# Cross attention: softmax sums by bf16 products of a split sum tile, taken four slots behind the pass

## Chip, cores, metric

One core of a Trainium2 chip. The metric is the device time of one execution in microseconds. The kernel computes a whole decoder of two layers; the change touches the cross attention of the second one.

## The reference, cut to what matters

The cross attention of layer 1 has 4 batch rows of 256 query tokens, 16 query heads in 4 groups of key and value heads, head size 128, and 1857 keys (the 256 tokens themselves and 1601 of context). Queries and keys are projected, normalised and rotated. Then, per head:

```python
scores = jnp.einsum('bhqd,bhkd->bhqk', q, k) * SCALE
p = softmax(scores)                       # over the 1857 keys
out = jnp.einsum('bhqk,bhkd->bhqd', p, v)
x = x + out.reshape(B, S, H * HD) @ Wo.T
```

The kernel divides by the softmax sum at the end: what a head adds to x is multiplied by one over the sum of its exponentials.

## The kernel before, in words

The stage "stream" (`cross_stream`, line 1705 on) makes 32 **passes** (4 batch rows x 4 key heads x 2 halves, each half 2 query heads x 256 queries = 512 columns). A pass has 15 **steps**, one per tile of 128 keys (the last has 65). All engines run the same hand-written list of **slots**, one step a slot; each kind of work for step s stands in slot s plus a fixed delay, and every engine works its list in order:

- slot s: TensorE (PE) makes the scores of step s, three bf16 products of 512 columns (L1950), into bank s % 2. ScalarE (ACT) copies them to SBUF (L2038), into one of 22 rooms. VectorE (DVE) takes the running maximum (L2217, L2214 for the first two tiles) from the bank, and that frees the bank: the score of step s + 2 waits for the maximum of step s.
- 15 to 17 slots behind a pass's first: the maximum is transposed (L1958), reduced (L2235) and spread over a bank (L1965).
- slot s + 18: DVE lowers step s by the maximum (L2203), ACT takes its exponential (L2044).
- slot s + 20: GpSimd (POOL) adds the exponentials of step s to `acc`, an fp32 tile of 128x512, two of them by turns (L2145, L2142); PE multiplies them with the values (fp32, L1975) into bank 2 or 3, the bank of the weighed values of this pass.
- slot 15h + 35 and 36 of pass h: ACT and DVE split the weighed values in two bf16 halves, `att` (L2086, L2271).
- slot 15h + 36: PE sums `acc` over its partitions (`sum_up`, L1983): four fp32 products with a column of ones, each 128 weights wide and one column long, into bank 6. The profile shows each as two records. DVE takes the reciprocal (L2277). The last pass has a form of its own (L1989).
- slots 15h + 40 and 41: PE multiplies `att` with the output weights (L2004), DVE adds to x with the reciprocals (L2288). Bank 6 is shared by the transposed maxima, turned queries and keys, sums and output products, each waiting until the one before it is taken.

Between these, every five slots a **unit** of the next key head's projections begins: products in slots 0 to 3 of the unit (L1893), ACT's squares (L2054) and copies of the values (L2070), DVE's rotations (L2262, L2263), POOL's sums and norms (L2152, L2158, L2163), and later the transposes (L1935), ACT's L2080 and DVE's L2267. The pattern of slots repeats every two passes, so even and odd passes see different neighbours.

Wo is loaded in the first four groups through `raw`, a tile of 128x1024 fp32: 4 loads of 512 KB on SP's queue (`out_weights`), each split by ACT (L2115) and in two parts by DVE (L2329). Context chunks (`ctx_chunk`) share the queue.

Of the kernel before, what the change touches and what calls it, by code (L numbers as in the profile page):

```python
# [8 lines left out]
ALU = mybir.AluOpType  # L9
# [1576 lines left out]
SUM_LATE = ATT_LATE + 1  # L1586
OUT_LATE = 2 * STEPS + 10

# [45 lines left out]
def cross_attention(nc, x, const, a, w, kept, first_row, experts):  # L1634

    with Stage(nc, "cross") as keep:
# [6 lines left out]
        less = sb("less", [P, P], BF16)  # L1643
        half = sb("half", [P, 4])
# [5 lines left out]
        with Stage(nc, "cross_w") as st:  # L1650
# [8 lines left out]
            with nc.Block() as block:  # L1659
                @block.gpsimd  # L1660
                def _(gp):
                    nc.gpsimd.memset(ones[:], 1.0)
                    nc.gpsimd.memset(less[:], -1.0)
                    nc.gpsimd.memset(half[:], -0.5)
                    nc.gpsimd.memset(eps[:], 1e-6)
# [35 lines left out]
        cross_stream(nc, x, const, a, w, experts, w_q, w_kv, w_o, k_gain, q_gain, freq, ones, less, half, eps, own_t, in_t, ctx_t,  # L1701
# [3 lines left out]
def cross_stream(nc, x, const, a, w, experts, w_q, w_kv, w_o, k_gain, q_gain, freq, ones, less, half, eps, own_t, in_t, ctx_t,  # L1705
                 where, where_f, angle, turns, sin, k_tab, q_tab, raw):

    with Stage(nc, "stream") as st:
# [17 lines left out]
        raw_o = raw[:].rearrange("p (h n) -> p h n", h=REP)  # L1726
# [120 lines left out]

        with nc.Block() as block:
            @block.sync
            def _(sp):  # L1850
                def out_weights(k):
                    if k >= 1:
                        sp.wait_ge(wo_lo, 2 * k)
                    sp.dma_start(raw_o, w["Wo"].rearrange("(k h p) n -> k p h n", p=P, h=REP)[k]).then_inc(wo_loaded, 16)
# [7 lines left out]
                for b in range(1, BATCH):  # L1862
# [20 lines left out]
            def _(pe):  # L1883
# [83 lines left out]
                def weigh(step):  # L1967
# [5 lines left out]
                    if t == 0 and h >= 2:  # L1973
                        pe.wait_ge(att_lo, h - 1)
                    nc.tensor.matmul(ps[:, 2 + n, :], v[0:r, g % 2, t, :], room(step)[0:r],  # L1975
                                     start=(t == 0), stop=(t == KT - 1)).then_inc(weighed, 1)

                def sum_up(h):
                    wait_bank6("sum", h)
                    if h < LAST:  # L1980
                        pe.wait_ge(acc_ready, after_first(STEPS * (h + 1) - 1))
                        for c in range(4):
                            last = nc.tensor.matmul(ps[:, 6, c:c + 1], acc[:, h % 2, c * P:(c + 1) * P], ones[:], start=True, stop=True)  # L1983
                    else:
                        pe.wait_ge(acc_ready, after_first(STEPS * h + REST - 1))
# [733 lines left out]
```

## Time and profile before

| | us |
|---|---|
| median of 3 runs | 1640.0 |
| lowest, highest | 1637.98, 1640.43 |
| profiled execution | 1639.1 |
| its span, first to last instruction | 1637.1 |

The stream runs from about 460 to 1556 us of the span. Times in the rows are microseconds from the span's start unless marked ns. PE is the matmuls, PEld the weight loads of the same engine, which can run beside earlier matmuls. In the timelines the first number is the start, the second the time until the end; consecutive matmuls overlap in their tails, so the distance between two starts is what a matmul costs the engine. A bracket at the end is idle time of the engine and what ended it.

### The profile page before, as it was taken

How to read it: one execution, taken by the hardware profiler on the slowest of the kernel's cores; microseconds unless marked ns; L12 is line 12 of the kernel's file. 1: busy time of each engine (PE TensorE's matmuls, PEld its weight loads, DVE VectorE, ACT ScalarE, POOL GpSimd, SP SyncE). 2: the span in 40 equal slices, each digit the busy share in tenths (PEclk: the TensorE clock that was granted, in tenths of full speed). 3: DMA queues.
4: the chain of work that ended last, by engine and by line, in shares of the span. 5: the costliest groups of instructions: out<-in, count | busy, mean ns of one | idle time of the engine just before them, and what ended most of it. 6: DMA issues, size and time to landing. Idle time of an engine off the chain costs nothing. (4 is left out here: it accounts for less than half of the span.)

```text
span 1637.1 us, 25648 instructions
## 1 busy us (share of the span) xinstructions
PE 1462.8 (89%) x8204; PEld 847.8 (52%) x8204; DVE 1305.8 (80%) x2612; ACT 1022.6 (62%) x2407; POOL 1133.5 (69%) x1034
## 2 busy tenths in 40 slices
PE   6598697758779999899999999989989999999988
PEld 5477465433444555455455555545545555554455
DVE  7876576878669888888978888888888888888865
ACT  3364464744366877677677767677666766767552
POOL 2364462112458889988878998878899888887742
PEclk9799798879899999999999999999999999999999
DMA  3000841020100001000000000000000000000020
GB/s 103 1 3 2 280 133 39 1 74 0 33 1 14 12 3 35 20 1 1 1 1 1 28 14 1 1 1 1 14 28 1 1 1 1 1 1 0 1 59 27
DMA packets 30974, 38.45 MB, mean 23 GB/s; under 512 B 4980, under 2 KB 26488, under 8 KB 30840
## 3 DMA queue, kind: packets, MB, share of 16 engines
q1 hardware_dynamic: 30840, 36.82, 7.0%
q8 instruction: 66, 1.08, 0.3%
q14 instruction: 68, 0.56, 0.1%
HBM read 35.76 MB, written 1.05 MB: 22 GB/s over the span
## 5 line engine op out<-in xcount | busy, mean ns | idle before, releaser
L2145 POOL TENSOR_TENSOR stream_acc<-stream_acc,stream_weights 128x512 f32<-128x512 f32 (+1 forms) x374 | 491.9, 1315 | 74.2 <-ACT stream_weights L2044 52.3
L1975 PE MATMUL stream_banks<-stream_weights,stream_v 128*128 128x512 f32 (+1 forms) x876 | 450.0, 598 | 0.0
L2038 ACT COPY stream_weights<-stream_banks 128x512 f32<-128x512 f32 (+1 forms) x438 | 255.8, 584 | 226.7 <-PE stream_banks L1950 216.8
L2217 DVE TENSOR_TENSOR stream_most<-stream_most,stream_banks 128x512 bf16<-128x512 bf16 (+1 forms) x416 | 284.7, 684 | 138.4 <-ACT stream_weights L2038 124.0
L2044 ACT ACTIVATE stream_weights<-stream_weights 128x512 f32<-128x512 f32 (+1 forms) x438 | 278.0, 635 | 66.6 <-DVE stream_weights L2203 62.8
L2203 DVE TENSOR_TENSOR stream_weights<-stream_weights,stream_banks 128x512 f32<-128x512 f32 (+1 forms) x438 | 296.8, 680 | 1.9 <-PE stream_banks L1965 0.6
L1950 PE MATMUL stream_banks<-stream_q_t_hi,stream_k_t_hi 128*128 128x512 bf16 (+1 forms) x480 | 183.1, 381 | 15.4 <-DVE stream_most L2217 13.9
L2152 POOL TENSOR_TENSOR stream_by_cos<-stream_by_cos,stream_by_sin 128x256 f32<-128x256 f32 x192 | 135.8, 728 | 79.0 <-DVE stream_by_sin L2263 79.0
L1950 PE MATMUL stream_banks<-stream_q_t_hi,stream_k_t_lo 128*128 128x512 bf16 (+1 forms) x480 | 182.8, 381 | 0.0
L1950 PE MATMUL stream_banks<-stream_q_t_lo,stream_k_t_hi 128*128 128x512 bf16 (+1 forms) x480 | 182.8, 381 | 0.0
L1975 PEld LDWEIGHTS stream_banks<-stream_weights,stream_v 128*128 128x128 f32 (+1 forms) x876 | 145.2, 191 | 29.8 <-issue 4.3
L1950 PEld LDWEIGHTS stream_banks<-stream_q_t_lo,stream_k_t_hi 128*128 128x128 bf16 (+1 forms) x480 | 47.5, 99 | 138.8 <-issue 135.0
L1950 PEld LDWEIGHTS stream_banks<-stream_q_t_hi,stream_k_t_hi 128*128 128x128 bf16 (+1 forms) x480 | 47.2, 98 | 138.2 <-issue 102.5
L2163 POOL TENSOR_TENSOR stream_normed<-stream_by_cos,row_ctx_t 128x512 f32<-128x512 f32 x96 | 100.1, 1043 | 8.4 <-PE stream_banks L1935 1.1
L2054 ACT ACTIVATE stream_squares<-stream_banks 128x128 bf16<-128x128 f32 x368 | 96.7, 276 | 8.2 <-PE stream_banks L1893 8.0
L2158 POOL TENSOR_TENSOR row_ctx_t<-row_ctx_t,cross_half 128x4 f32<-128x4 f32 x96 | 100.4, 1046 | 0.0
L1893 PE MATMUL stream_banks<-early_w_kv_hi,row_in_t_hi 128*128 128x256 bf16 x416 | 79.5, 273 | 5.1 <-DVE stream_by_sin L2263 5.1
L1893 PE MATMUL stream_banks<-early_w_kv_lo,row_in_t_hi 128*128 128x256 bf16 x416 | 79.5, 273 | 0.0
L1893 PE MATMUL stream_banks<-early_w_kv_hi,row_in_t_lo 128*128 128x256 bf16 x416 | 79.4, 273 | 0.0
L2054 ACT ACTIVATION_READ_ACCUMULATOR stream_squares<-stream_banks 128x1 f32 x368 | 76.9, 209 | 0.0
L1950 PEld LDWEIGHTS stream_banks<-stream_q_t_hi,stream_k_t_lo 128*128 128x128 bf16 (+1 forms) x480 | 47.4, 99 | 56.8 <-issue 0.8
L1893 PEld LDWEIGHTS stream_banks<-early_w_kv_hi,row_in_t_hi 128*128 128x128 bf16 x416 | 40.2, 98 | 52.5 <-DVE stream_by_sin L2263 7.1
(443 smaller groups left out, 3097.6 us busy)
## 6 DMA issues: line engine op xcount, KB each, us to landing
memory_raw_t<-in_ctx_t SPq DMA_DIRECT2D x4, 1601.0 KB, 8.9
memory_raw<-in_ctx SPq DMA_DIRECT2D x4, 1536.0 KB
row_ctx_t<-in_ctx_t SPq DMA_DIRECT2D x6, 512.0 KB, 3.6
early_raw<-in_L_xattn_Wq SPq DMA_DIRECT2D x4, 512.0 KB, 3.8
early_raw<-in_L_xattn_Wo SPq DMA_DIRECT2D x4, 512.0 KB, 3.9
row_ctx_t<-in_ctx_t SPq DMA_DIRECT2D x1, 1601.0 KB, 6.9
moe_raw_up<-in_L_ffn_wi SPq DMA_DIRECT2D x6, 256.0 KB, 4.9
model_x<-in_x SPq DMA_DIRECT2D x1, 1024.0 KB, 5.6
```

The costliest lines, as they stand in the source:

```text
L1893: last = nc.tensor.matmul(out, rows, moving(two, c), start=(n == 0), stop=(n == 3 * DC - 1))
L1950: last = nc.tensor.matmul(ps[0:r, step % 2, :], k_t[one][:, t * P:t * P + r], q_t[two][:, g % 2, PAIR * n:PAIR * (n + 1), :], start=(one = ...
L1975: nc.tensor.matmul(ps[:, 2 + n, :], v[0:r, g % 2, t, :], room(step)[0:r], start=(t == 0), stop=(t == KT - 1)).then_inc(weighed, 1)
L2038: nc.scalar.copy(room(step)[0:r], ps[0:r, step % 2, :]).then_inc(copied, 1)
L2044: nc.scalar.activation(room(step)[0:r], room(step)[0:r], ACT.Exp, scale=SCALE).then_inc(p_ready, 1)
L2054: last = nc.scalar.activation(squares[:, h, :], heads[:, h - some.start, :], ACT.Square, accum_out=ss[:, u % 2, h:h + 1])
L2145: nc.gpsimd.tensor_tensor(acc[0:r, h % 2, :], acc[0:r, h % 2, :], room(step)[0:r], ALU.add).then_inc(acc_ready, 1)
L2152: last = nc.gpsimd.tensor_tensor(by_cos[:, u % 2, 0:n, to], by_cos[:, u % 2, 0:n, to], by_sin[:, u % 2, 0:n, of], ALU.add)
L2158: nc.gpsimd.tensor_tensor(rms[:, u % 2, 0:n], var[:, u % 2, 0:n], half[:, 0:n], ALU.pow).then_inc(rms_ready, 1)
L2163: nc.gpsimd.tensor_tensor(normed[:, 0:n], by_cos[:, u % 2, 0:n], bcast(rms[:, u % 2, 0:n], 2, HD), ALU.mult).then_inc(normed_ready, 1)
L2203: nc.vector.tensor_tensor(room(step)[0:r], room(step)[0:r], ps[0:r, 7, :], ALU.add).then_inc(lowered, 1)
L2217: nc.vector.tensor_tensor(most[0:r], most[0:r], ps[0:r, step % 2, :], ALU.max).then_inc(maxed, 1)
```

## The change

The sum of a pass h < 31 is now made from two bf16 halves of `acc`. In slot 15h + 38 ACT copies `acc` to a bf16 tile and DVE subtracts it from `acc` into a second one, the rounding rest. In slot 15h + 39 PE makes eight bf16 products with a bf16 column of ones, two per 128 queries, accumulated, into the bank of the weighed values of the pass (2 or 3), which `att` has freed by then. The reciprocal moves to the same slot, and the next pass but one waits for it before it weighs into that bank. Bank 6 no longer holds sums, but for the last pass's. The two halves lie in the second half of `raw`, so that Wo now comes in 8 loads of 256 KB through the first half, and its splits and their slots move (ACT at slots 8 and 17 of a group, DVE at 12 and 22). ACT's `split_high` stands right behind its exponential of the slot, DVE's `split_low` right behind its running maximum.

```diff
+SPLIT_LATE = SUM_LATE + 2
+def sums_in(slot):
+    return [h for h in pass_at(slot, SPLIT_LATE + 1) if h < PASSES - 1] + [h for h in pass_at(slot, SUM_LATE) if h == PASSES - 1]
+def splits_in(slot):
+    found = [("sum", h) for h in pass_at(slot, SPLIT_LATE) if h < PASSES - 1]
+    return found
...
-        raw_o = raw[:].rearrange("p (h n) -> p h n", h=REP)
+        raw_o = raw[:, 0:512].rearrange("p (h n) -> p h n", h=2)
+        halves = [raw[:, 512 + 256 * i:768 + 256 * i].bitcast(BF16) for i in range(2)]
...
-                                ("sum", pass_at(s, SUM_LATE)), ("out", outs_in(s))):
+                                ("sum", sums_in(s)), ("out", outs_in(s))):
                 for item in items:
-                    if kind == "out" and item[0] == PASSES - 1:
+                    if kind == "out" and item[0] == PASSES - 1 or kind == "sum" and item < PASSES - 1:
                         continue
...
                 def out_weights(k):
                     if k >= 1:
-                        sp.wait_ge(wo_lo, 2 * k)
-                    sp.dma_start(raw_o, w["Wo"].rearrange("(k h p) n -> k p h n", p=P, h=REP)[k]).then_inc(wo_loaded, 16)
+                        sp.wait_ge(wo_lo, k)
+                    sp.dma_start(raw_o, w["Wo"].rearrange("(k h p) n -> k p h n", p=P, h=2)[k]).then_inc(wo_loaded, 16)
...
                     if b == 1:
-                        out_weights(1)
-                        out_weights(2)
+                        for k in range(1, 6):
+                            out_weights(k)
                     ctx_chunk(b, 2)
                     if b == 1:
-                        out_weights(3)
+                        out_weights(6)
                     ctx_chunk(b, 3)
+                    if b == 1:
+                        out_weights(7)
...
                     if t == 0 and h >= 2:
                         pe.wait_ge(att_lo, h - 1)
+                        pe.wait_ge(inv_ready, h - 1)
...
                 def sum_up(h):
-                    wait_bank6("sum", h)
                     if h < LAST:
-                        pe.wait_ge(acc_ready, after_first(STEPS * (h + 1) - 1))
+                        pe.wait_ge(att_lo, h + 1)
+                        pe.wait_ge(split_lo, split_at["sum", h] + 1)
                         for c in range(4):
-                            last = nc.tensor.matmul(ps[:, 6, c:c + 1], acc[:, h % 2, c * P:(c + 1) * P], ones[:], start=True, stop=True)
+                            for part in range(2):
+                                last = nc.tensor.matmul(ps[:, 2 + h % HALVES, c:c + 1], halves[part][:, c * P:(c + 1) * P], ones_b[:],
+                                                        start=(part == 0), stop=(part == 1))
                     else:
+                        wait_bank6("sum", h)
...
+                def split_high(kind, n):
+                    if kind == "sum":
+                        ac.wait_ge(acc_ready, after_first(STEPS * (n + 1) - 1))
...
+                    if split_at[kind, n] >= 1:
+                        kind_before, before = splits[split_at[kind, n] - 1]
+                        if kind_before == "sum":
+                            ac.wait_ge(sum_ready, before + 1)
...
+                    nc.scalar.copy(split_part(kind, n, 0), split_source(kind, n)).then_inc(split_hi, 1)
...
-                    if 0 <= g < KVH and late == 8:
-                        ac.wait_ge(wo_loaded, 16 * (g + 1))
-                        nc.scalar.copy(w_o[0][:, REP * g:REP * (g + 1), :], raw_o).then_inc(wo_hi, 1)
+                    if 0 <= g < KVH and late in (8, 17):
+                        k = 2 * g + late // 17
+                        ac.wait_ge(wo_loaded, 16 * (k + 1))
+                        nc.scalar.copy(w_o[0][:, 2 * k:2 * k + 2, :], raw_o).then_inc(wo_hi, 1)
...
+                def split_low(kind, n):
+                    ve.wait_ge(split_hi, split_at[kind, n] + 1)
+                    nc.vector.tensor_tensor(split_part(kind, n, 1), split_source(kind, n), split_part(kind, n, 0), ALU.subtract).then_inc(split_lo, 1)
...
-                    nc.vector.reciprocal(inv[:, 4 * n:4 * n + 4], ps[:, 6, 0:4]).then_inc(inv_ready, 1)
+                    nc.vector.reciprocal(inv[:, 4 * n:4 * n + 4], ps[:, 6 if h == LAST else 2 + n, 0:4]).then_inc(inv_ready, 1)
...
-                    if 0 <= g < KVH and late in (17, 22):
-                        some = slice(0, 2) if late == 17 else slice(2, 4)
-                        ve.wait_ge(wo_hi, g + 1)
...
+                    if 0 <= g < KVH and late in (12, 22):
+                        k = 2 * g + late // 22
+                        ve.wait_ge(wo_hi, k + 1)
```

## Rows read from the trace of the kernel before

**Rows 1.** Part 1 of the page, busy time of each engine.

```profile
PE 1462.8 (89%) x8204; PEld 847.8 (52%) x8204; DVE 1305.8 (80%) x2612; ACT 1022.6 (62%) x2407; POOL 1133.5 (69%) x1034
```

**Rows 2.** The table by stretch: busy us of PE, PEld, DVE, ACT, POOL; clock.

```profile
1300.00:1400.00 100.00, 99.98 (x507) 55.54 (x505) 83.26 (x155) 69.03 (x190) 83.90 (x79) 1.00 0.00 1
```

**Rows 3.** Groups by line, 500 to 1560 us: busy us, mean ns, idle before.

```profile
L1983 PEld LDWEIGHTS stream_banks<-cross_ones,stream_acc 128*128 128x128 f32 x248 | 31.2, 192 | 6.5 <-issue 4.5
L1983 PE MATMUL stream_banks<-cross_ones,stream_acc 128*128 128x1 f32 x248 | 29.7, 241 | 2.6 <-POOL stream_acc L2145 2.6
```

**Rows 4.** Timeline of PE, an even pass: start us, us, engine, line.

```profile
1012.22 0.95 PE L1983 MATMUL stream_banks<-cross_ones,stream_acc 128*128 128x1 f32 x8
1013.03 1.10 PE L1975 MATMUL stream_banks<-stream_weights,stream_v 128*128 128x512 f32 x2
1013.97 0.38 PE L1950 MATMUL stream_banks<-stream_q_t_hi,stream_k_t_hi 128*128 128x512 bf16 x1
...
1014.62 1.02 PE L1975 MATMUL stream_banks<-stream_weights,stream_v 128*128 128x512 f32 x2
1015.61 0.38 PE L1950 MATMUL stream_banks<-stream_q_t_hi,stream_k_t_hi 128*128 128x512 bf16 x1
...
1019.38 1.02 PE L1975 MATMUL stream_banks<-stream_weights,stream_v 128*128 128x512 f32 x2
...
1032.34 0.39 PE L1958 MATMUL stream_banks<-model_ident_b,stream_most 128*128 128x128 bf16 x4
1032.56 1.08 PE L1975 MATMUL stream_banks<-stream_weights,stream_v 128*128 128x512 f32 x2
```

**Rows 5.** Timeline of PE's weight loads, same stretch.

```profile
1013.54 0.10 PEld L1950 LDWEIGHTS stream_banks<-stream_q_t_hi,stream_k_t_hi 128*128 128x128 bf16 x1 [0.24 <-issue]
...
1015.58 0.10 PEld L1950 LDWEIGHTS stream_banks<-stream_q_t_hi,stream_k_t_hi 128*128 128x128 bf16 x1 [0.77 <-issue]
```

**Rows 6.** Timeline of DVE, same stretch.

```profile
1014.78 0.68 DVE L2217 TENSOR_TENSOR stream_most<-stream_most,stream_banks 128x512 bf16<-128x512 bf16 x1
...
1019.55 0.69 DVE L2217 TENSOR_TENSOR stream_most<-stream_most,stream_banks 128x512 bf16<-128x512 bf16 x1 [0.35 <-ACT stream_weights L2038]
...
1021.71 0.69 DVE L2217 TENSOR_TENSOR stream_most<-stream_most,stream_banks 128x512 bf16<-128x512 bf16 x1 [0.87 <-ACT stream_weights L2038]
```

**Rows 7.** Timeline of ACT, the exponential at the slot of the split, even pass.

```profile
1017.50 0.63 ACT L2044 ACTIVATE stream_weights<-stream_weights 128x512 f32<-128x512 f32 x1
```

**Rows 8.** Timeline of POOL, same slot.

```profile
1018.43 1.27 POOL L2145 TENSOR_TENSOR stream_acc<-stream_acc,stream_weights 128x512 f32<-128x512 f32 x1
```

**Rows 9.** Line 2329 on DVE: count, then min/median/max ns.

```profile
L2329 DVE TENSOR_TENSOR cross_w_o_lo<-early_raw,cross_w_o_hi x8: 684/823/1281, 485.7 to 707.1; 128x512 bf16<-128x512 f32 x8
```

**Rows 10.** Timeline of DVE, one subtraction with both inputs in SBUF.

```profile
695.42 0.93 DVE L2329 TENSOR_TENSOR cross_w_o_lo<-early_raw,cross_w_o_hi 128x512 bf16<-128x512 f32 x1
```

**Rows 11.** Timeline of POOL beside it.

```profile
694.76 1.04 POOL L2163 TENSOR_TENSOR stream_normed<-stream_by_cos,row_ctx_t 128x512 f32<-128x512 f32 x1
695.76 1.73 POOL L2145 TENSOR_TENSOR stream_acc<-stream_acc,row_ctx_t 128x512 f32<-128x512 f32 x1
```

**Rows 12.** Timeline of PE, the output products of the same even pass.

```profile
1022.83 0.38 PE L1950 MATMUL stream_banks<-stream_q_t_hi,stream_k_t_lo 128*128 128x512 bf16 x1
1023.24 0.28 PE L2004 MATMUL stream_banks<-cross_w_o_hi,stream_att_hi 128*128 128x256 bf16 x1
```

**Rows 13.** Timeline of DVE, an odd pass.

```profile
1048.81 0.69 DVE L2217 TENSOR_TENSOR stream_most<-stream_most,stream_banks 128x512 bf16<-128x512 bf16 x1 [1.21 <-ACT row_ctx_t L2038]
```

**Rows 14.** Timeline of ACT, the exponential at its split slot.

```profile
1050.62 0.66 ACT L2044 ACTIVATE stream_weights<-stream_weights 128x512 f32<-128x512 f32 x1
```

**Rows 15.** Timeline of POOL, same slot.

```profile
1051.36 1.27 POOL L2145 TENSOR_TENSOR stream_acc<-stream_acc,stream_weights 128x512 f32<-128x512 f32 x1 [0.71 <-ACT stream_weights L2044]
```

**Rows 16.** Timeline of PE, where the odd pass's products would stand.

```profile
1052.75 1.02 PE L1975 MATMUL stream_banks<-stream_weights,stream_v 128*128 128x512 f32 x2
```

**Rows 17.** Timeline of PE, the same place of pass 29.

```profile
1518.44 1.02 PE L1975 MATMUL stream_banks<-stream_weights,stream_v 128*128 128x512 f32 x2
```

More of the change, by code:

```diff
@@ L1643, in cross_attention @@
         less = sb("less", [P, P], BF16)
+        ones_b = sb("ones_b", [P, 1], BF16)
         half = sb("half", [P, 4])
@@ L1662, in _ @@
                     nc.gpsimd.memset(ones[:], 1.0)
+                    nc.gpsimd.memset(ones_b[:], 1.0)
                     nc.gpsimd.memset(less[:], -1.0)
@@ L1699, in _, with cross_stream @@
                                                 own_t[0][:, :, tok], ALU.subtract)
-        cross_stream(nc, x, const, a, w, experts, w_q, w_kv, w_o, k_gain, q_gain, freq, ones, less, half, eps, own_t, in_t, ctx_t,
+        cross_stream(nc, x, const, a, w, experts, w_q, w_kv, w_o, k_gain, q_gain, freq, ones, ones_b, less, half, eps, own_t, in_t, ctx_t,
                      where, where_f, angle, turns, sin, k_tab, q_tab, kept["raw"])
-def cross_stream(nc, x, const, a, w, experts, w_q, w_kv, w_o, k_gain, q_gain, freq, ones, less, half, eps, own_t, in_t, ctx_t,
+def cross_stream(nc, x, const, a, w, experts, w_q, w_kv, w_o, k_gain, q_gain, freq, ones, ones_b, less, half, eps, own_t, in_t, ctx_t,
                  where, where_f, angle, turns, sin, k_tab, q_tab, raw):
@@ L1846, in cross_stream, with split_source, split_part @@
                              "out": lambda: (added, QT * (PAIR * item[0] + item[1] + 1))}[kind]()
+        split_hi, split_lo = sem("split_hi"), sem("split_lo")
+        splits = [item for s in SLOTS for item in splits_in(s)]
+        split_at = {item: n for n, item in enumerate(splits)}
+        def split_source(kind, n):
+            return acc[:, n % 2, :] if kind == "sum" else room(n)[0:rows_of(n % STEPS)]
+        def split_part(kind, n, part):
+            return halves[part] if kind == "sum" else halves[part][0:rows_of(n % STEPS)]
         with nc.Block() as block:
@@ L2017, in _ @@
                         turn(u)
-                    for h in pass_at(slot, SUM_LATE):
+                    for h in sums_in(slot):
                         sum_up(h)
@@ L2080, in high @@
                     nc.scalar.copy(place(0, u), turned_heads(u)).then_inc(hi_ready, 1)
+                def split_high(kind, n):
+                    if kind == "sum":
+                        ac.wait_ge(acc_ready, after_first(STEPS * (n + 1) - 1))
+                    else:
+                        ac.wait_ge(p_ready, n + 1)
+                    if split_at[kind, n] >= 1:
+                        kind_before, before = splits[split_at[kind, n] - 1]
+                        if kind_before == "sum":
+                            ac.wait_ge(sum_ready, before + 1)
+                        else:
+                            ac.wait_ge(weighed, before + 1)
+                    nc.scalar.copy(split_part(kind, n, 0), split_source(kind, n)).then_inc(split_hi, 1)
                 def att_high(h):
@@ L2092, in _ @@
                         exponent(slot - LOWER)
+                    for kind, n in splits_in(slot):
+                        split_high(kind, n)
                     for h in pass_at(slot, ATT_LATE):
@@ L2313, in _ @@
                         keep_most(slot)
+                    for kind, n in splits_in(slot):
+                        split_low(kind, n)
                     if 0 <= slot - WEIGH < ALL:
                         accumulate_rest(slot - WEIGH)
-                    for h in pass_at(slot, SUM_LATE):
+                    for h in sums_in(slot):
                         invert(h)
@@ L2325, in _ @@
                                                 in_t[0][:].rearrange("p c n -> p (c n)")[:, some], ALU.subtract).then_inc(pair_lo, 1)
[L2326 to L2329 removed]
+                    if 0 <= g < KVH and late in (12, 22):
+                        k = 2 * g + late // 22
+                        ve.wait_ge(wo_hi, k + 1)
+                        nc.vector.tensor_tensor(w_o[1][:, 2 * k:2 * k + 2, :], raw_o, w_o[0][:, 2 * k:2 * k + 2, :],
                                                 ALU.subtract).then_inc(wo_lo, 1)
```

1 line of the change is left out of this document (removed).

## The prediction, made before the change ran

> **What bounds the kernel now.** I read the busy shares first, then the table by stretch, then the groups by line, and last the timelines of all engines around two places: the old sum of a pass and the slot in which the change puts the split. TensorE (PE) is busy for 89% of the span [rows 1]. Inside the attention it is busy for 99.98 of 100 us at the full clock, with VectorE (DVE) at 83, GpSimd (POOL) at 84 and ScalarE (ACT) at 69 [rows 2]. So TensorE's own work sets the pace on average. An average hides single places, though, so I looked for slots in which TensorE stood behind another engine. The pattern repeats every two passes (30 slots); I take pass 14 (even) and pass 15 (odd).
>
> In an even pass there is such a place two slots behind the sum. The score of slot 38 of the pass (counting from its first score) starts at 1015.61 [rows 4]. It needs the running maximum of slot 36, which ends at 1014.78 + 0.68 = 1015.46 on VectorE [rows 6]. Its first weight load begins at 1015.58, only 0.03 before the product, whereas the one before it was loaded 0.43 ahead (1013.54 against 1013.97) [rows 4, 5]. The load waited for VectorE; 0.15 us is the delay from VectorE's end to the product. The maximum that frees the bank is 0.15 us ahead of this score in all 15 even passes but the last. So here TensorE arrives just in time, and an earlier TensorE would only wait. In odd passes it is not so: VectorE itself waits 1.21 us before its maximum in the slot behind the sum [rows 13], and no score of these slots has less than 1.4 us of slack.
>
> **Removed.** 31 of the 32 sums lose their fp32 products: 248 records of 31.2 us of loads and 29.7 us of products [rows 3]. On the path, one sum takes 1013.03 - 1012.22 = 0.81 us, and the weighing behind it 0.94 instead of the usual 0.86, for its fp32 load hides behind nothing (the 0.08 comes back behind the new sum). An odd pass gets the 0.81. An even pass gets nothing: the score at 1015.61 waits for VectorE as before. Passes 28 and 30 lie where projections have ended, so I credit them. That is 15 odd + 2 = 17 passes x 0.81 = **-13.8 us**; the other 14 get 0.
>
> **Added on TensorE.** 8 bf16 pairs a pass, of one column. No such row exists. From above: four bf16 transposes of 128 columns take 1032.56 - 1032.34 = 0.22 us, so eight pairs 0.44. From below: a share of it, down to some 0.2, since the loads could be less than half of it. I take 0.44, the nearest bf16 row: 31 x 0.44 = **+13.6 us**. The Trainium skill ("TensorE: Matmul & The Clock Gate", "Back-to-back issue gap") says that starts of products never come closer than about 25 ns; by that estimate eight take 0.2 us, the sum would be 7.4 us lower, and no row here shows which holds. In the 14 even passes without credit the 0.08 behind the sum is new: **+1.1 us**.
>
> **Added on ACT and DVE, and the wait.** ACT's copy of 128x512 from SBUF I price by the exponential, 0.63 us, the next instruction starting 0.53 behind its start [rows 7]. ACT is 69% busy, nothing of it counts by itself. But the copy stands behind the exponential, and DVE's subtraction behind the copy; everything behind both on their queues moves, and TensorE stands at the products.
>
> The subtraction reads both inputs from SBUF. Its like at line 2329 took 684 ns at least, 823 in the middle, 1281 at most [rows 9]; from PSUM the same shape takes 684. The difference has a cause in the trace: at 695.42 it was issued while a POOL product ran from 694.76 to 695.80, and it ended at 696.35, 0.55 behind POOL's end; POOL's next addition then took 1.73 instead of its usual 1.27 [rows 10, 11]. Whoever starts first holds the other up. The Trainium skill ("SBUF — State Buffer", "Who interferes with whom") has this as a rule: a VectorE instruction with two SBUF inputs contends with a GpSimd one that reads SBUF, and the later one blocks fully. It speaks against this change, and the rows agree.
>
> Even pass: VectorE no longer has the reciprocal at the old place (0.2 us), so ACT's exponential starts 0.2 earlier, at 1017.30. Copy at 1017.83 to 1018.46, subtraction wanted at 1018.5. But POOL began an accumulation at 1018.43 - 0.2 = 1018.23, which holds until 1019.50 [rows 8]. The subtraction ends 0.55 later, 1020.05, and the products can start at 1020.20. TensorE would want them at 1019.38, where its weighing now stands [rows 4]. **Wait 0.82 us.** Unblocked, it would end at 1019.2 and cost nothing.
>
> Odd pass: exponential at 1050.62, copy 1051.15 to 1051.78, POOL's accumulation 1051.36 to 1052.63, subtraction until 1053.18, products at 1053.33, TensorE there at 1052.75 [rows 14 to 16]: **wait 0.58 us** (all of it shifts together by the 0.81).
>
> Going through the 28 passes 0 to 27 in this way on POOL's timeline, 12 even and 12 odd ones have the accumulation in that place; four have a shorter instruction or an earlier end there, and no wait. Pass 29 has no projections beside it: the same chain would let the products start at 1520.3, TensorE is there at 1518.44 [rows 17], 1.9 us. Together 12 x 0.82 + 12 x 0.58 + 1.9 = **+18.7 us**.
>
> What is late next: DVE goes on some 1.7 us later. It has 0.35 + 0.87 us of idle time before the maxima of the next two slots [rows 6], and TensorE is itself 0.82 + 0.44 us late, so the scores find their banks free; and the second output product, which now waits 1023.24 - 1022.83 - 0.22 = 0.2 us for DVE's addition [rows 12], no longer does: 12 x -0.2 = **-2.4 us**. The wait for `inv_ready` ahead of a weighing comes eleven slots after the reciprocal: nothing. Eight loads of Wo of half the size, their copies and subtractions: the same eight subtractions, and the first loads are needed five slots after they are freed; the context chunk queued behind the fifth of them on SP is freed at slot 72 and needed at slot 83. Nothing, covered by those slots; if DMA were late, one stall of a few us at most.
>
> **Sum.** -13.8 + 13.6 + 1.1 + 18.7 - 2.4 = +17.2 us. The profiled execution took 1639.1 us (span 1637.1 and 2.0 around it), 0.9 below the median of 1640.0. 1639.1 + 17.2 = **1656 us**.
>
> **Rivals.**
> - *No wait.* The subtraction slips in ahead of POOL's accumulation, or POOL's shift frees it. Waits and the 2.4 fall away: +0.9, 1640; with pairs at 0.2 us a sum 1633. For it: 0.27 us decide the order in even passes. Against: in odd ones 0.4 us do. Chance 0.15, half within 0.2%, half faster.
> - *TensorE's work alone counts* (the other sign): the place in even passes moves because VectorE's work before it is shifted too, and no wait shows: 31 x (0.44 - 0.81) = -11.5, 1628; at 0.2 us, 1620. It decides if the maximum of slot 36 ends over 0.4 us earlier. Against it stands 0.15 us of slack in every even pass. Chance 0.09.
> - *VectorE becomes the bound.* It has 0.7 us more work and up to 0.9 us of standing per pass in the stretch where it has least idle time; should odd passes lose their credit as well, +31, 1670. It decides if odd slack, 1.4 us, is used up. Chance 0.12.
> - That the edit does not act as told I rule out: the split stands four slots behind the last accumulation and the sums leave bank 6 in the code.
>
> **Numbers.** Forecast 0.64, its own range 1646 to 1664. About 0.2% (3 us) is what a measurement of this kernel can tell from no change. Faster: 0.08 of the no-wait case and 0.09, 0.17. Same: its other 0.07 and 0.02 from the low edge of the forecast, 0.09. Slower: 0.62 + 0.12 = 0.74. The range 1635 to 1667 takes in the forecast with pairs at 0.2 us (1649), most of the no-wait case and half of the VectorE case.
>
> **What would show it.** Right: the groups of the new products wait for DVE's subtraction, about 0.6 us on average and in all 15 to 20 us; the subtraction has a mean near 1.4 to 1.6 us, not 0.69; the score two slots behind the old sum waits some 0.8 us in even passes. Eight pairs take 0.2 to 0.44 us. Wrong: a mean of the subtraction near 0.7, or TensorE's idle time before the products near zero, or no new idle time before the score of slot 38.

## The result and the profile after

The changed kernel takes 1663.7 us (median of 4 runs, 1661.6 to 1664.7) against 1640.2 (4 runs, 1638.0 to 1641.4): a ratio of 1.0143, 95% interval 1.0126 to 1.0161. It is slower, by 23.5 us; 1656 was forecast, range 1635 to 1667. The profiled execution took 1664.7 us, its span 1662.9.

Part 1 of the page, which answers to [rows 1]:

```profile
PE 1449.2 (87%) x8095; PEld 829.8 (50%) x8204; DVE 1343.2 (81%) x2643; ACT 1043.7 (63%) x2442; POOL 1143.0 (69%) x1035
```

TensorE's products are busy 13.6 us less than before, and the span is 25.8 us longer. (The 13.6 are rough: both kernels have 8204 weight loads, but the trace after has only 8095 products, so 109 records of products are missing from it.) From the first product of the stream to its last weighing it is 1136.1 us instead of 1111.2, 24.9 more. So it isn't more work on TensorE; the time went into its waiting and, in part, into a lower clock. The table of waits of TensorE, who waited for whom, us in total, times, longest, first of the kernel before and then of the one after:

```profile
PE stream_banks L1950 <- DVE stream_most L2217: 13.9, 14, 1.5
...
PE stream_banks L1983 <- POOL stream_acc L2145: 2.6, 3, 0.9
...
PE stream_banks L2004 <- DVE model_x L2288: 0.6, 1, 0.6
```

```profile
PE stream_banks L1979 <- DVE stream_most L2266: 29.1, 23, 3.2
PE stream_banks L2014 <- DVE early_raw L2320: 22.4, 26, 2.1
...
PE stream_banks L2037 <- DVE model_x L2341: 3.4, 14, 0.2
```

L1979 are the scores (L1950 before), L2014 the new products on the halves in `raw`, L2037 the output products. Two waits have grown: the scores wait 29.1 instead of 13.9 us for VectorE's running maximum, the sums 22.4 instead of 2.6. The 3.4 instead of 0.6 us of the output products is no growth; it comes from missing records, as the timeline of pass 14 shows below. The table also counts a wait from the modelled end of the product before, which lies 0.16 us behind the moment at which the next one could start. Where it matters I count from start to start instead, with the missing products put in at their usual cost. The new products and the subtraction itself, by source line (min/median/max ns; then who they waited for):

```profile
L2014 PE MATMUL stream_banks<-cross_ones_b,early_raw x248: 163/163/167, 541.3 to 1565.9; 128*128 128x1 bf16 x124
```

```profile
L2320 DVE TENSOR_TENSOR early_raw<-stream_acc,early_raw x31: 692/1542/1789, 539.4 to 1564.9; 128x512 bf16<-128x512 f32 x31
...
  ACT early_raw L2126: 14.9, 31
```

The middle (median) subtraction takes 1542 ns, against 684 to 693 for one that nothing holds up.

**The even pass.** Timeline of TensorE in pass 14, which answers to [rows 4]:

```profile
1031.19 0.38 PE L1979 MATMUL stream_banks<-stream_q_t_hi,stream_k_t_hi 128*128 128x512 bf16 x1 [0.86 <-DVE stream_most L2266]
...
1034.32 0.38 PE L1922 MATMUL stream_banks<-early_w_q_lo,cross_own_t_hi 128*128 128x512 bf16 x1
1034.54 0.59 PE L1922 MATMUL stream_banks<-early_w_q_hi,cross_own_t_lo 128*128 128x512 bf16 x2
1035.77 0.34 PE L2014 MATMUL stream_banks<-cross_ones_b,early_raw 128*128 128x1 bf16 x8 [0.64 <-DVE early_raw L2320]
1035.97 1.10 PE L2005 MATMUL stream_banks<-stream_weights,stream_v 128*128 128x512 f32 x2
1036.91 0.38 PE L1979 MATMUL stream_banks<-stream_q_t_hi,stream_k_t_hi 128*128 128x512 bf16 x1
...
1039.29 0.38 PE L1979 MATMUL stream_banks<-stream_q_t_lo,stream_k_t_hi 128*128 128x512 bf16 x1
1039.91 0.28 PE L2037 MATMUL stream_banks<-cross_w_o_hi,stream_att_hi 128*128 128x256 bf16 x1 [0.24 <-DVE model_x L2341]
```

A weight load of TensorE in the same place:

```profile
1039.29 0.10 PEld L1979 LDWEIGHTS stream_banks<-stream_q_t_hi,stream_k_t_lo 128*128 128x128 bf16 x1
```

Timeline of VectorE, then of POOL, and last POOL's next two additions in the kernel before:

```profile
1034.05 1.58 DVE L2320 TENSOR_TENSOR early_raw<-stream_acc,early_raw 128x512 bf16<-128x512 f32 x1 [0.54 <-ACT early_raw L2126]
1035.55 0.68 DVE L2252 TENSOR_TENSOR stream_weights<-stream_weights,stream_banks 128x512 f32<-128x512 f32 x1
```

```profile
1032.39 2.69 POOL L2194 TENSOR_TENSOR stream_acc<-stream_acc,stream_weights 128x512 f32<-128x512 f32 x2 [0.52 <-ACT stream_weights L2077]
1035.03 1.88 POOL L2201 TENSOR_TENSOR stream_by_cos<-stream_by_cos,stream_by_sin 128x256 f32<-128x256 f32 x2
```

```profile
1019.66 1.41 POOL L2152 TENSOR_TENSOR stream_by_cos<-stream_by_cos,stream_by_sin 128x256 f32<-128x256 f32 x2
```

The score of slot 38 starts at 1031.19 after 0.86 us of idle time: the old sum has gone from ahead of it, and TensorE stands there instead. The subtraction is issued at 1034.05, waits for the second of POOL's two additions (until 1032.39 + 2.69 = 1035.08) and ends at 1035.63, 0.55 later; the products start at 1035.77, 0.15 behind that. TensorE could have started them at 1034.54 + 2 x 0.22 = 1034.97, so it lost 0.80 us. The eight products then take 1035.97 - 1035.77 = 0.20 us. The second output product behind them, at 1039.91, still waits as before. The third product of the score ahead of it has left its weight load (1039.29) but no record; with it the wait is 1039.91 - 1039.29 - 2 x 0.22 = 0.19 us (0.187 unrounded), the same as the 0.19 in [rows 12]. The record is missing at this place in 13 passes, and that makes the 3.4 us of the table. POOL's next two additions (L2201) take 1.88 us together instead of 1.41, as the subtraction holds them up in turn.

**The odd pass.** Timeline of TensorE in pass 25 (of the kind of [rows 16]), then POOL's after and before in the same slots:

```profile
1415.08 0.38 PE L1922 MATMUL stream_banks<-early_w_kv_hi,row_in_t_lo 128*128 128x256 bf16 x2
1416.05 0.34 PE L2014 MATMUL stream_banks<-cross_ones_b,early_raw 128*128 128x1 bf16 x8 [0.58 <-DVE early_raw L2320]
1416.25 1.10 PE L2005 MATMUL stream_banks<-row_ctx_t,stream_v 128*128 128x512 f32 x2
```

```profile
1409.83 2.69 POOL L2194 TENSOR_TENSOR stream_acc<-stream_acc,stream_weights 128x512 f32<-128x512 f32 x2
1412.66 2.69 POOL L2194 TENSOR_TENSOR stream_acc<-stream_acc,row_ctx_t 128x512 f32<-128x512 f32 x2
```

```profile
1388.68 2.68 POOL L2145 TENSOR_TENSOR stream_acc<-stream_acc,stream_weights 128x512 f32<-128x512 f32 x2
1391.68 1.28 POOL L2145 TENSOR_TENSOR stream_acc<-stream_acc,row_ctx_t 128x512 f32<-128x512 f32 x1 [0.32 <-ACT row_ctx_t L2044]
1393.66 1.27 POOL L2145 TENSOR_TENSOR stream_acc<-stream_acc,row_ctx_t 128x512 f32<-128x512 f32 x1 [0.70 <-ACT row_ctx_t L2044]
```

Here TensorE loses 1416.05 - 1415.30 = 0.75 us. Before, POOL stood idle for 0.32 and 0.70 us ahead of two of these additions; after, TensorE comes 0.89 us earlier and the idle times are gone: POOL is already behind and can't follow, so its last addition ends at 1415.35 and the subtraction at 1415.90.

From the sum of pass 24 to that of pass 26, two passes, it was 1420.54 - 1354.51 = 66.03 us before and is 1449.79 - 1382.54 = 67.25 after. The even one of a pair costs 0.80 + 0.20 + 0.08 = 1.08 us, with nothing gained; the odd one 0.75 + 0.20 + 0.08 - 0.89 = 0.14. That is the 1.22.

**The three even passes with a wait for POOL, and the clock.** In passes 4, 12 and 20 the old sum itself waited for POOL. Pass 4 before, at the sum and at the score two slots on, then a stretch behind that score (busy us of PE, PEld, DVE, ACT, POOL; the first number behind them is the granted clock):

```profile
668.45 1.02 PE L1983 MATMUL stream_banks<-cross_ones,stream_acc 128*128 128x1 f32 x8 [0.87 <-POOL stream_acc L2145]
...
673.27 0.38 PE L1950 MATMUL stream_banks<-stream_q_t_hi,stream_k_t_hi 128*128 128x512 bf16 x1 [1.32 <-DVE stream_most L2217]
```

```profile
674.00:676.00 2.00, 2.00 (x11) 1.00 (x10) 2.00 (x4) 1.91 (x4) 2.00 (x4) 1.00 0.00 0
```

The same score after, and a stretch behind it:

```profile
680.54 0.58 PE L1979 MATMUL stream_banks<-stream_q_t_hi,stream_k_t_hi 128*128 128x512 bf16 x1 [3.23 <-DVE stream_most L2266]
680.92 0.63 PE L1979 MATMUL stream_banks<-stream_q_t_lo,stream_k_t_hi 128*128 128x512 bf16 x1
681.35 0.63 PE L1979 MATMUL stream_banks<-stream_q_t_hi,stream_k_t_lo 128*128 128x512 bf16 x1
```

```profile
681.00:683.00 2.00, 2.00 (x6) 0.73 (x5) 1.55 (x3) 1.61 (x3) 2.00 (x3) 0.50 0.00 0
```

With the old sum gone, its wait joins that of the score, which is now 3.39 us from start to start. Behind it the granted clock is 0.50 (1.2 instead of 2.4 GHz), and the products of the score start 0.43 us apart instead of 0.22. The same happens behind the 3.39 us of pass 12, not behind those of pass 20. Between 445 and 1556 us the trace after has seven such stretches at the lower clock and the trace before has three. Counted from start to start their products cost 11.0 us more than at the full clock, against 4.8 before: 6.3 of the 24.9 us (from unrounded figures). No experiment here changed the clock alone, so this part is read from the traces only.

### The profile page after: what moved, and what is told of

The parts are those of the page before. It is cut to its first block and busy times, and to the rows that moved or that the text cites. A ratio compares the mean times of both kernels' runs of the same rounds, so it can differ in the third digit from the quotient of the medians.

```text
span 1662.9 us, 25643 instructions
## 1 busy us (share of the span) xinstructions
PE 1449.2 (87%) x8095; PEld 829.8 (50%) x8204; DVE 1343.2 (81%) x2643; ACT 1043.7 (63%) x2442; POOL 1143.0 (69%) x1035
## 3 DMA queue, kind: packets, MB, share of 16 engines
q8 instruction: 66, 1.08, 0.3%
## 5 line engine op out<-in xcount | busy, mean ns | idle before, releaser
L2201 POOL TENSOR_TENSOR stream_by_cos<-stream_by_cos,stream_by_sin 128x256 f32<-128x256 f32 x192 | 140.3, 751 | 94.3 <-DVE stream_by_sin L2312 94.3
L1979 PE MATMUL stream_banks<-stream_q_t_lo,stream_k_t_hi 128*128 128x512 bf16 (+1 forms) x479 | 182.8, 382 | 4.2 <-DVE stream_most L2266 0.3
L1979 PE MATMUL stream_banks<-stream_q_t_hi,stream_k_t_hi 128*128 128x512 bf16 (+1 forms) x405 | 154.6, 382 | 30.3 <-DVE stream_most L2266 28.8
L1979 PE MATMUL stream_banks<-stream_q_t_hi,stream_k_t_lo 128*128 128x512 bf16 (+1 forms) x463 | 177.0, 382 | 0.1
L1979 PEld LDWEIGHTS stream_banks<-stream_q_t_hi,stream_k_t_hi 128*128 128x128 bf16 (+1 forms) x480 | 47.4, 99 | 156.7 <-issue 123.0
L1979 PEld LDWEIGHTS stream_banks<-stream_q_t_lo,stream_k_t_hi 128*128 128x128 bf16 (+1 forms) x480 | 47.5, 99 | 137.2 <-issue 133.4
L1922 PE MATMUL stream_banks<-early_w_kv_hi,row_in_t_hi 128*128 128x256 bf16 x416 | 79.5, 273 | 5.6 <-DVE stream_by_sin L2312 5.6
L1922 PE MATMUL stream_banks<-early_w_kv_hi,row_in_t_lo 128*128 128x256 bf16 x416 | 79.4, 273 | 0.0
L1922 PE MATMUL stream_banks<-early_w_kv_lo,row_in_t_hi 128*128 128x256 bf16 x416 | 79.4, 273 | 0.0
L1979 PEld LDWEIGHTS stream_banks<-stream_q_t_hi,stream_k_t_lo 128*128 128x128 bf16 (+1 forms) x480 | 47.5, 99 | 56.9 <-issue 1.1
L219 POOL TENSOR_TENSOR self_sm<-self_sm,self_mx 128x512 f32<-128x512 f32 (+1 forms) x32 | 47.0, 1470 | 28.8 <-DVE self_mx L312 28.8
```

Of the source, the lines that this page charges most:

```text
L1922: last = nc.tensor.matmul(out, rows, moving(two, c), start=(n == 0), stop=(n == 3 * DC - 1))
L1979: last = nc.tensor.matmul(ps[0:r, step % 2, :], k_t[one][:, t * P:t * P + r], q_t[two][:, g % 2, PAIR * n:PAIR * (n + 1), :], start=(one = ...
L2201: last = nc.gpsimd.tensor_tensor(by_cos[:, u % 2, 0:n, to], by_cos[:, u % 2, 0:n, to], by_sin[:, u % 2, 0:n, of], ALU.add)
```

## The experiments

In short, the theory: (a) the products stand behind a VectorE instruction that POOL holds up; (b) in even passes taking the old sum away gains nothing. Rivals: VectorE's or ACT's extra work as such sets the time; TensorE's work alone counts. Waits "ahead of the sums" are counted from TensorE's timeline as the start of the first product less the start of the matmul before it less what that one costs (0.22 us for 512 columns, 0.11 for 256); they are 26.8 us in the changed kernel, 3.1 in the one before. Where the matmul before it is a weighing, it costs 0.43 us. Each experiment's ratio is to runs of the kernel before in the same series, whose medians are 1639.3 to 1640.0 us.

### One SBUF input for the subtraction

```diff
-                    nc.vector.tensor_tensor(split_part(kind, n, 1), split_source(kind, n), split_part(kind, n, 0), ALU.subtract).then_inc(split_lo, 1)
+                    nc.vector.tensor_tensor(split_part(kind, n, 1), ps[:, 2 + n % HALVES, :], split_part(kind, n, 0), ALU.subtract).then_inc(split_lo, 1)
```

> The changed kernel with the subtraction reading its first input from PSUM (the weighed values, so the sums are not those of the exponentials) instead of acc in SBUF: the same shape, place and waits, but one SBUF input. Theory: it no longer stands behind GpSimd's addition and takes 0.69 us in all passes instead of 1.54; the wait of the products falls from 0.8 to about 0 in even passes and to under 0.1 in odd ones; in all 17 to 21 us less, 1643 to 1647. Rival (the queue place or ACT's copy sets the wait): the subtraction still ends late, time stays at 1660 or more.

1644.5 us, ratio to the kernel before 1.0036 (1.0019 to 1.0052). The subtraction by source line:

```profile
L2320 DVE TENSOR_TENSOR early_raw<-stream_banks,early_raw x31: 691/692/693, 538.9 to 1544.4; 128x512 bf16<-128x512 f32 x31
```

It takes 692 ns in all 31 passes, and the waits ahead of the sums fall from 26.8 to 7.7 us. Of these 3.3 are in passes 1, 3 and 5 and 4.2 in the last three; in the rest there is practically none. Place, shape, order and every wait in the code are the same, only the second SBUF input is gone. That shows (a): with what follows from it, it is some 19 of the 23.5 us. The last three passes are another matter: with the subtraction at 0.69 us the waits of passes 28 and 30 are still 0.85 and 2.0 us, as in the changed kernel, and that of pass 29 is 1.35 instead of 2.24.

### The products one slot later

```diff
-    return [h for h in pass_at(slot, SPLIT_LATE + 1) if h < PASSES - 1] + [h for h in pass_at(slot, SUM_LATE) if h == PASSES - 1]
+    return [h for h in pass_at(slot, SPLIT_LATE + 2) if h < PASSES - 1] + [h for h in pass_at(slot, SUM_LATE) if h == PASSES - 1]
```

> The changed kernel with the products one slot later (two slots behind the split instead of one); nothing else moves. Theory (the products stand waiting for VectorE's subtraction, which stands behind an addition on GpSimd): the wait of 0.75 to 0.95 us per pass goes, as a slot is 2.2 us; about 24 of the 26.8 us of waits vanish. VectorE stays 1.5 us late, so the second output product of even passes waits up to 0.4 us longer (about +5). Time 1638 to 1646. Rival (the path is lost elsewhere, by VectorE's extra work as such): stays above 1655.

1658.8 us (1.012, 1.0103 to 1.0137): only 5 less, and the forecast of 1638 to 1646 failed. The waits ahead of the sums did go (1.7 left), but TensorE's table of waits shows where most of them went:

```profile
PE stream_banks L1922 <- DVE stream_by_sin L2312: 18.6, 15, 2.0
...
PE stream_banks L2037 <- DVE model_x L2341: 7.1, 14, 1.0
...
PE stream_banks L2014 <- DVE early_raw L2320: 1.4, 2, 0.8
```

The projections (L1922) now wait 18.6 us for VectorE's rotations (L2312), which stand behind the subtraction on its queue, against 6.0 before; the output products wait 7.1, and from start to start 11.6 against 4.1 before. So the delay of VectorE by some 1.6 us is itself more than the slots have room for; the wait at the products had hidden the next one (this is read from the trace; no run tests it apart). Moving the consumer is no cure where the queue behind the slow instruction is short of slack too.

### Fewer products in even passes alone, in odd passes alone

The kernel before with one of the four products of its sum, in even passes alone; the second kernel has `h % 2 == 1` in the same place.

```diff
-                        for c in range(4):
+                        for c in range(1 if h % 2 == 0 and 1 <= h < 28 else 4):
```

> The kernel before, with one of the four fp32 sum products left out to one in the even passes 2 to 26 (13 passes; three quarters of those sums aren't computed). Takes 0.61 us of TensorE's work away per pass. Theory (the score two slots behind waits for VectorE's maximum, slack 0): no gain, 1640 within 2. Rival (TensorE's own work is all that counts): 13 x 0.61 = 8 us less, 1632.

> The same cut in the odd passes 1 to 27 (14 passes). Theory (1.4 us of slack there): full gain, 14 x 0.61 = 8.5 us less, 1631 to 1632. Rival (VectorE bounds both kinds): no gain, 1640.

Odd: 1629.5 us, 0.9943 (0.9925 to 0.9962), 9.7 us less. The trace gives 0.67 us a pass, 14 x 0.67 = 9.4; I had expected 0.61. Even: 1644.9 us, 1.0041 (1.0027 to 1.0055), no gain, rather a loss. The profiled execution of it took 1639.3. From the sum of pass 22 to that of pass 26 it is 132.06 us in both kernels, though two sums in between are 0.67 us shorter each. The wait of the scores for VectorE's maximum grew by the work taken away. As its timed runs lay above the profiled one, it ran again:

> The kernel of e3_even_cut again, on another chip job, since its timed runs lay 4 us above its profiled one: three quarters of the sums of the even passes 2 to 26 aren't computed. Theory: no gain, within 0.2% of the kernel before (1640). Rival: 8 us less.

1645.0 us, 1.0033 (1.0021 to 1.0045), profiled 1639.7:

```profile
PE stream_banks L1950 <- DVE stream_most L2217: 21.7, 24, 2.0
```

21.7 against 13.9 us, 7.8 more. The cut is in truth 13 x 0.67 = 8.7 us, and counted from start to start in the first of the two traces, products at the lower clock left out, the idle time ahead of the scores grows by 9.0 (28.7 against 19.7). That shows (b). The 5 us by which the timed runs are longer have no trace; their mean granted clock is 0.954 to 0.961 where the runs of the kernel before beside it have 0.959 to 0.965. Within the twelve runs the longest (1647.7) has 0.956 and the shortest (1638.5) 0.961. That fits the clock as the cause, but does not show it.

### The fp32 sum moved, nothing split

The changed kernel with a wait for `acc` and the four old products on it in the new place, and no split.

```diff
-    return found
+    return []
...
-                        pe.wait_ge(split_lo, split_at["sum", h] + 1)
+                        pe.wait_ge(acc_ready, after_first(STEPS * (h + 1) - 1))
                         for c in range(4):
-                            for part in range(2):
-                                last = nc.tensor.matmul(ps[:, 2 + h % HALVES, c:c + 1], halves[part][:, c * P:(c + 1) * P], ones_b[:],
-                                                        start=(part == 0), stop=(part == 1))
+                            last = nc.tensor.matmul(ps[:, 2 + h % HALVES, c:c + 1], acc[:, h % 2, c * P:(c + 1) * P], ones[:], start=True, stop=True)
```

> The changed kernel with the four fp32 products on acc itself, at the new place (slot 39, bank of the weighed values), and no split at all. Theory: in the 14 even passes taking the sum from slot 36 gains nothing (TensorE then waits for VectorE's maximum) and putting it into slot 39 costs all of its 0.89 us, +12.5; in odd passes -0.89 and +0.89 cancel; the 3.1 us of waits before three old sums go. 1649. Rival (the same work in another slot costs the same): 1640.

1656.2 us, 1.0106 (1.0089 to 1.0123), 16 us slower with the same instructions as before and no split. The even passes lose 0.89 us each between their scores, as expected (12.5), odd ones nothing. The 3.1 us of waits ahead of three old sums did not come back, as these too lie in even passes, ahead of the score that waits for VectorE; in the trace the stream is 13.8 us longer in all, and 2.8 us more lie behind its last weighing, where nothing was changed. So moving the sum away from the place where it was free costs its whole length. This 16 us is not a share of the changed kernel's loss: there the sum costs 0.28 us in its new place and not 0.89, which over the 14 even passes is 3.9 us.

### The price of the pairs

```diff
-                            for part in range(2):
+                            for part in (0, 1, 0, 1, 0, 1):
```

> The changed kernel with every bf16 pair of products made three times (16 more pairs a pass; the column ends with the same sums). Prices the pairs: at 25 ns each, as the trace after shows them (0.20 us for eight), 31 x 0.40 = 12.4 us more than the changed kernel, 1676. Rival (55 ns each, as the transposes of 128 columns): +27, 1691. If they hid behind something: 1664.

1679.1 us, 15.4 more than the changed kernel; in the trace both kinds of passes are 0.40 us longer, 16 pairs at 25 ns, 12.4 us in all. The other 3 us go with a lower granted clock of this kernel (0.953 against 0.959 in the profiled executions): its products at the lower clock cost 15.0 us more than at the full one, against 11.0 in the changed kernel.

### Wo's second subtraction four slots later

```diff
-                    if 0 <= g < KVH and late in (12, 22):
-                        k = 2 * g + late // 22
+                    if 0 <= g < KVH and late in (12, 26):
+                        k = 2 * g + late // 26
```

> The changed kernel with the second subtraction of Wo in slot 26 of its group instead of 22, one slot ahead of the split of odd passes. Theory (two subtractions with both inputs in SBUF close together, each held up by GpSimd): the wait of the products in passes 1, 3 and 5 falls from 1.65 to 1.9 us to the 0.75 of the later odd passes, about 3 us less: 1661. Rival (the first groups wait longer for another reason): unchanged, 1664.

1661.8 us, 1.9 less, which the timing cannot tell for sure (the intervals, 1.0121 to 1.0152 and 1.0126 to 1.0161, overlap). The trace shows the waits themselves: those of passes 1, 3, 5 go from 1.64, 1.89, 1.65 to 0.0, 1.43, 0.0 us (I had expected 0.75). From the sum of pass 0 to that of pass 7 it is 2.9 us shorter; behind it 2.0 us are lost again, 0.7 of them because pass 21 waits here. In the changed kernel pass 1 shows the reason, on VectorE's timeline:

```profile
572.84 1.68 DVE L2384 TENSOR_TENSOR cross_w_o_lo<-early_raw,cross_w_o_hi 128x512 bf16<-128x512 f32 x1
...
576.32 1.35 DVE L2320 TENSOR_TENSOR early_raw<-stream_acc,early_raw 128x512 bf16<-128x512 f32 x1 [0.61 <-ACT early_raw L2126]
```

The subtraction of Wo also reads two inputs from SBUF, takes 1.68 us one slot ahead, and makes the split late: ACT's exponential, behind which its copy for the split stands, waits for VectorE. Pass 3 keeps most of its wait; that stays open.

### Only the odd passes as changed

The changed kernel with the split in passes 1, 3, ... 27; all others have the old sum in slot 36, in bank 6. The same set decides which bank the reciprocal reads.

```diff
+SPLIT_PASSES = range(1, 28, 2)
...
+    return [h for h in pass_at(slot, SPLIT_LATE + 1) if h in SPLIT_PASSES] + [h for h in pass_at(slot, SUM_LATE) if h not in SPLIT_PASSES]
...
+    found = [("sum", h) for h in pass_at(slot, SPLIT_LATE) if h in SPLIT_PASSES]
```

> The changed kernel with the even passes and the last four back to the fp32 sum in slot 36; only the odd passes 1 to 27 are split. Theory: each even pass in steady state cost 1.09 us (0.80 wait, 0.20 products, 0.08 load, no gain), 14 x 1.09 = 15, and the ends 29 and 30 about 3.5 more: 1645. Rival (even and odd passes share the loss): above 1652.

1641.3 us, 1.0009 (0.9997 to 1.0021). Putting the even passes and the ends back takes 22 us away, more than the 18.5 expected; the odd ones by themselves come out even within what the timing can tell.

### A version that keeps what was to be had

First, the split in odd passes 7 to 27 only, so that Wo's loads stay as in the kernel before; `acc` is lifted to PSUM by a second ACT copy in slot 37, so that the subtraction has one SBUF input; the sums stand in slot 39, as in the changed kernel.

```diff
+SPLIT_PASSES = range(7, 28, 2)
...
+                    nc.scalar.copy(ps[:, 2 + n % HALVES, :], split_source(kind, n)).then_inc(split_kept, 1)
...
-                    nc.vector.tensor_tensor(split_part(kind, n, 1), split_source(kind, n), split_part(kind, n, 0), ALU.subtract).then_inc(split_lo, 1)
+                    nc.vector.tensor_tensor(split_part(kind, n, 1), ps[:, 2 + n % HALVES, :], split_part(kind, n, 0), ALU.subtract).then_inc(split_lo, 1)
```

> The kernel before, with the split only in the odd passes 7 to 27 (11 passes), and its subtraction reading acc from PSUM, where ACT copies it a slot earlier: one SBUF input, nothing of GpSimd to wait for. Wo, even passes and the ends are as before. Theory: each of the 11 gives 0.89 - 0.20 - 0.08 = 0.61 us, 6.7 in all: 1633. Rival (ACT's two copies and VectorE's lateness take it back): 1638 or more.

1640.1 us, 1.0004 (0.9994 to 1.0013); missed. The subtraction takes 692 ns, but the lift makes ACT's copies of the scores 0.5 us late in the very slot, and the products wait 0.50 us in eight of the 11 passes, 0.68 to 0.73 in the others (9.2 us in all with the three waits ahead of fp32 sums). Its profiled execution, at 1635.5 us, was the shortest of its eleven, so this trace is not of a middle one. Then the same work in the holes of the queues: both ACT copies at the end of its list for slot 36, the subtraction on VectorE in slot 37 ahead of the running maximum, the eight products in slot 38.

```diff
+    return [h for h in pass_at(slot, SUM_LATE + 2) if h in SPLIT_PASSES] + [h for h in pass_at(slot, SUM_LATE) if h not in SPLIT_PASSES]
...
+    found = [("sum", h) for h in pass_at(slot, SUM_LATE) if h in SPLIT_PASSES]
...
+                    for kind, n in splits_in(slot):
+                        split_high(kind, n)
+                        split_lift(kind, n)
...
+                    for kind, n in splits_in(slot - 1):
+                        split_low(kind, n)
```

> As v1_odd_lifted (only odd passes 7 to 27 split, acc lifted to PSUM), but ACT's two copies stand at the end of its slot 36, ahead of 1.8 us in which it stood idle, VectorE's subtraction ahead of its maximum in slot 37, where it stood 1.2 us, and the products in slot 38. Theory: then neither engine is late and the 0.5 us that the products still waited go: 11 x 0.61 = 6.7 us less than before, 1633. Rival (what comes off the odd passes is lost behind them): 1638 or more.

1634.5 us (8 runs) against 1639.9 (25), 0.9968 (0.9954 to 0.9981): 5.4 us faster than the kernel before, and the lowest time of the kernels that compute all of their sums. The same slots of pass 25, TensorE and VectorE:

```profile
1388.30 0.60 PE L1965 MATMUL stream_banks<-model_ident,stream_normed 128*128 128x128 f32 x4
1388.73 0.34 PE L2021 MATMUL stream_banks<-cross_ones_b,early_raw 128*128 128x1 bf16 x8
1388.94 1.10 PE L2007 MATMUL stream_banks<-stream_weights,stream_v 128*128 128x512 f32 x2
```

```profile
1386.43 0.69 DVE L2333 TENSOR_TENSOR early_raw<-stream_banks,early_raw 128x512 bf16<-128x512 f32 x1
1387.04 0.68 DVE L2278 TENSOR_TENSOR stream_most<-stream_most,stream_banks 128x512 bf16<-128x512 bf16 x1
```

The products follow the transposes at once (1388.73 is 0.43 behind the first of four), with no idle time; the subtraction takes 0.69 us and ends 1.6 us ahead of them. In the trace each of the passes is 0.89 - 0.28 = 0.61 us shorter, as expected.

## Why the prediction was right, and where its sizes were off

**Direction and cause** held: TensorE waits in the new place for a subtraction, and the products follow 0.15 us behind it wherever TensorE waits, in 26 of 31 passes. In 24 of these the subtraction ends 0.55 us behind a POOL addition that held it up; in passes 28 and 30 it takes 0.69 us and nothing holds it. The waits of the even passes were forecast as 0.82 and are 0.80.

**Removed: 17 passes credited, 14 not.** Right in kind (even cut: nothing, odd cut: all). Missed: three even passes (4, 12, 20) had 1.0 us of wait for POOL ahead of the old sum, and that went the same way, into the wait for VectorE. It costs nothing by itself, as the same 3.1 us stood ahead of the sums before, but it is a gain that did not come, and it makes the 3.39 us waits behind two of which the clock fell.

**Added: 13.6 us at 55 ns a pair.** The failed term: it is 25 ns a pair, 0.20 us a pass, 31 x 0.20 = 6.2, so 7.4 too much. That is what the sentence on the Trainium skill ("TensorE: Matmul & The Clock Gate", "Back-to-back issue gap") gave; the row of 128-column transposes was the wrong neighbour.

**Waits: 18.7 us.** The changed kernel has 26.8. (1) "All of it shifts together by the 0.81" is false: POOL has only 0.3 and 0.7 us of slack there and stays behind, 0.75 instead of 0.58. (2) Passes 1, 3 and 5 wait 1.6 to 1.9 us; I took the move of Wo's subtractions for free, by counting them and not by asking what they do to the queue right behind. (3) The ends: pass 28 waits 0.86, pass 30 2.0, pass 29 2.2; I had only 1.9 for pass 29. (4) Which passes escape was read off a timeline that shifts: 4, 12, 15 and 21 do, and 20 nearly (0.07 us); in the traces with three times the pairs and with Wo's subtraction moved pass 21 waits too.

**The 2.4 us recovered** at the second output product did not come: each of these waits is 0.19 us, as before. I took TensorE to be late there and VectorE not. But the addition stands behind a running maximum that waits for ACT's copy of TensorE's own score ([rows 6], 0.87 us of idle time before). When TensorE is late, the score, the maximum and the addition are late with it.

**The clock** was not in the sum: 6.3 us, as told above. **Luck** has a part in the number: +17.2 was forecast and 25.6 measured between the profiled executions, and the error stays that small because 7.4 us too much for the pairs stand against 8.1 too little for the waits, 2.4 that did not come back and 6.3 of the clock. 17.2 - 7.4 + 8.1 + 2.4 + 6.3 = 26.6, against 24.9 in the stream.

**No wait** as a rival is refuted by the subtraction's length, **TensorE's work alone** by the even cut. **VectorE becomes the bound** holds a part that I had priced apart: in the changed kernel it shows little, but once the products are moved out of its way its delay comes back in the rotations (13 us there). The forecast would have been wrong about the cure.

Added up on TensorE from start to start, the sum is: -27.6 (31 x 0.89) + 8.7 (31 x 0.28) + 23.7 (waits ahead of the sums, 26.8 - 3.1) + 15.5 (waits of the scores, 35.2 - 19.7) + 6.3 (products at the lower clock) = 26.6. The output products add nothing. The stream is 24.9 us longer; the 1.7 less are waits that are shorter elsewhere, 1.2 of them ahead of the transposes (L1964). The 15.5 us are what (b) asks for: 14 x 0.89 from the even passes and 3.1 from the old waits for POOL, 15.6.

## What to carry to other kernels

Before work is taken off the busiest engine, look at each place it stands: where its next instruction already starts 0.15 us behind another engine's, nothing is gained, and moving the work out of such a place costs its whole length elsewhere. Look also at where two waits join into a longer one: behind two of three such places the clock was lower here. A VectorE instruction with two SBUF inputs beside a busy GpSimd must be priced with what is left of GpSimd's instruction, and again for all that stands behind it; one of the inputs in PSUM cures it. A new dependent step belongs into the idle stretches of the engines' own lists, found row by row, not into the slot where its data are due.

## What the runs showed of the hardware

Bf16 pairs of a weight load of 128 columns and a product of one column start 25 ns apart (0.20 us for eight, 0.60 for 24), a quarter of the fp32 form's 101 ns per record (0.81 us for eight). POOL's hold is seen in both directions: VectorE's 0.69 us became up to 1.79, POOL's pair of additions 1.88 instead of 1.41. With one input in PSUM the subtraction took 691 to 693 ns in all 31 passes. The granted clock of TensorE was 0.50 behind waits of 3.39 us (passes 4 and 12) and stayed at the full level behind a third of the same length (pass 20). And the kernel with the even cut had, in both of its series, mostly a lower mean granted clock in the timed runs than the kernel before beside it (0.954 to 0.961 against 0.959 to 0.965) and a median 5 us above its profiled execution; in which stretch is not shown.
